# Token-major Wo and W2 products and a new order around W1 in an eight-layer attention stack

## Chip, cores, metric

One core of one Trainium2 chip. The metric is the device time of one execution in microseconds, the median over runs.

## The reference

x is 16 sequences of 128 tokens of 256. After a layer norm it goes through eight layers of linear attention and feed-forward, then a cross attention and a mixture of experts, which the change does not touch. All is float32. One layer:

```
Q  = elu(x Wq + bq) + 1;  K = elu(x Wk + bk) + 1;  V = x Wv + bv        (16 heads of 64)
KV = sum over tokens of K * V;  sumK = sum over tokens of K             (elementwise)
att = Q * KV / (Q * sumK + 1e-6)
y  = gelu(att Wo + bo);  x = layer_norm(y + x)                          (1024 -> 256)
h  = gelu(x W1 + b1);    h = gelu(h W2 + b2);  x = layer_norm(h + x)    (256 -> 1024 -> 256)
```

## The kernel before, in words

A tile is four sequences, 512 tokens; there are 4 tiles a layer and 8 layers, 32 tiles. Channels lie in chunks of 128 on the partitions ("feature-major", 128 x 512 tokens) or tokens lie on the partitions ("token-major", four blocks of 128 tokens x 256 channels). The Q, K, V and W1 products split operands into a high and a low part (float32r) and add three products per 128-channel half of the input (`split_product`, lines 328 to 334): high by high, high by low, low by high. The Wo and W2 products (`down`, line 377) are plain float32, which TensorE runs as two passes.

Work goes in slots, all engines with the same loop. Slot t finishes tile t (its Wo product, layer norm, W1), starts tile t+1 (Q, K, V for four pairs of chunks) and makes the W2 product of tile t-1. Each engine has its order written out by hand in its own function `slot` and waits on semaphores for the others:

- TensorE (line 402): pair 0 (K, Q, V), half of Wo's product, pair 1, its other half (`y_mm`), pair 2's K and Q, transposes of gelu(y) to token-major (`to_tm`, line 374), pair 2's V, half of W2's product, pair 3, most of its other half, transposes of the normed x into PS (line 448), the last three chunks of W2's product (`z_mm`), transposes of the input two tiles on (`input_fm`, line 365), W1's eight products (`hidden`), transposes of gelu(z). PS has six banks: two for K, two for Q, two for V; W1's products go round the last four, so that its fifth needs the first to be freed by ScalarE's gelu (`h_act`).
- ScalarE (line 565): per pair relu of K and Q (`clip_keys`, `clip_queries`) and one exponential over both (line 507), then Ln and exponential for the reciprocal (`invert`, lines 515, 517), then ATT from eight scaled pieces (`weigh`, line 530). Gelu needs another function table than Ln and exponential, so that a slot loads tables four times. Copies of the high parts: `X1HI` (line 594), `XTHI` (line 540).
- VectorE (line 715): per pair `features` (the snap of the exponential, line 625, then two K features, line 631, and two Q features, line 635), `sums_of` (two products by V, line 645, and a reduction, line 650), `denominators` (line 663), `newton` (lines 675, 677); for x the residual (line 693), statistics and `normed` (line 711), the low parts (lines 682, 687).
- GpSimd: rstd, scale and shift of both layer norms, and twelve weight pieces a layer that it splits in parts (lines 249, 251), in the slots with t = 2 and t = 4.
- SyncE issues all loads of the next layer as buffers come free.

## Time and profile before

| | |
|---|---|
| median of 3 runs | 3143.17 us (3138.88 to 3148.4) |
| the profiled execution | 3142.58 us |
| its span, first to last instruction | 3140.5 us |
| mean granted TensorE clock | 0.965 |
| TensorE, VectorE, ScalarE, GpSimd busy | 93%, 73%, 59%, 29% |

The attention stack takes the first 2580 us or so. Idle time of an engine is printed in brackets with the engine and line that ended it. A matmul's printed time holds the way through the array, so consecutive ones overlap; their spacing is the cost. "issue" means that the profile shows nothing the engine waited for.

### The profile page before, as it was taken

To read this page: it belongs to the slowest core of one execution; us is meant where nothing else is said; L and a number is where in the kernel's file an instruction comes from. 1 tells how busy PE (TensorE), PEld (TensorE's weight loads), DVE (VectorE), ACT (ScalarE), POOL (GpSimd) and SP (SyncE) were. 2 spreads that over 40 slices of the span, in tenths; PEclk is the share of its full clock that TensorE was granted. 3 is DMA by queue.
4 is the path that set the end of the run, shared out by engine and by line. 5 is a ranking of instruction groups with operands and counts; after the bars stand their busy time and mean duration, and the time that the engine had idled before them with its cause. 6 is when DMAs were issued, how large, how long until landed. Compare 5 with 4: busy or idle time off the path is not lost. (4 is left out here: it accounts for less than half of the span.)

```text
span 3140.5 us, 34598 instructions
## 1 busy us (share of the span) xinstructions
PE 2925.5 (93%) x11342; PEld 1984.7 (63%) x11343; DVE 2305.1 (73%) x3334; ACT 1863.0 (59%) x2796; POOL 922.0 (29%) x590
## 2 busy tenths in 40 slices
PE   5799999999999999999999989999999977997995
PEld 4566666566666666666666656666666635775563
DVE  6878888888887888788888788878787826763111
ACT  4566777677767776777677767776777713441121
POOL 5005231523152315231513151315131133323002
PEclk8899999999999999999999999999999988996998
DMA  4000000000000000100000000000000008000012
GB/s 129 1 1 26 28 17 19 27 28 17 19 26 28 17 19 27 28 17 19 27 28 17 19 26 28 17 19 26 28 17 4 0 1 273 0 0 22 14 45 77
DMA packets 59658, 92.82 MB, mean 30 GB/s; under 512 B 14960, under 2 KB 38768, under 8 KB 57424
## 3 DMA queue, kind: packets, MB, share of 16 engines
q1 hardware_dynamic: 56832, 83.27, 8.4%
q0 software_dynamic: 2640, 7.21, 0.7%
q8 instruction: 99, 1.62, 0.2%
q14 instruction: 87, 0.71, 0.1%
HBM read 80.24 MB, written 10.22 MB: 29 GB/s over the span
## 5 line engine op out<-in xcount | busy, mean ns | idle before, releaser
L331 PE MATMUL PS<-XTHI,WHI 128*128 128x512 f32 x1536 | 652.7, 425 | 47.9 <-DVE EX L631 32.7
L333 PE MATMUL PS<-XTHI,WLO 128*128 128x512 f32 x1536 | 611.8, 398 | 0.0
L332 PE MATMUL PS<-XTLO,WHI 128*128 128x512 f32 x1536 | 611.7, 398 | 0.0
L256 POOL TENSOR_TENSOR RSTD<-MV,EPS 128x4 f32<-128x4 f32 x68 | 41.2, 606 | 1529.6 <-DVE MV L703 1524.0
L381 PE MATMUL Y<-H,W2S 128*128 128x512 f32 x1024 | 461.2, 599 | 2.7 <-DVE R L693 2.7
L381 PE MATMUL Y<-ATT,WO 128*128 128x512 f32 x1024 | 451.7, 594 | 4.1 <-ACT ATT L530 2.7
L530 ACT ACTIVATE ATT<-INV,CC,CE 128x128 f32<-128x128 f32 x1024 | 425.0, 481 | 2.6 <-DVE INV L677 2.6
L331 PEld LDWEIGHTS PS<-XTHI,WHI 128*128 128x128 f32 x1536 | 293.2, 191 | 140.1 <-issue 56.0
L332 PEld LDWEIGHTS PS<-XTLO,WHI 128*128 128x128 f32 x1536 | 293.1, 191 | 83.1 <-issue 20.3
L495 ACT ACTIVATE EX<-PS,BNEG 128x512 f32<-128x512 f32 x256 | 169.8, 686 | 288.4 <-PE PS L333 286.1
L381 PEld LDWEIGHTS Y<-ATT,WO 128*128 128x128 f32 x1024 | 194.7, 190 | 226.2 <-issue 215.5
L333 PEld LDWEIGHTS PS<-XTHI,WLO 128*128 128x128 f32 x1536 | 292.5, 190 | 69.3
L381 PEld LDWEIGHTS Y<-H,W2S 128*128 128x128 f32 x1024 | 194.2, 192 | 212.8 <-issue 204.3
L650 DVE TENSOR_REDUCE SUMS<-EX 128x16 f32<-128x2048 f32 x128 | 292.4, 2284 | 3.3
L625 DVE TENSOR_SCALAR EX<-EX 128x2048 f32<-128x2048 f32 x128 | 224.0, 1750 | 49.8 <-ACT EX L507 49.8
L507 ACT ACTIVATE EX<-EX 128x2048 f32<-128x2048 f32 x128 | 245.3, 1916 | 4.1
L663 DVE TENSOR_TENSOR EX<-EX,ES 128x1024 f32<-128x1024 f32 x128 | 236.2, 1845 | 5.5
L675 DVE TENSOR_TENSOR EX<-EX,INV 128x1024 f32<-128x1024 f32 x128 | 165.0, 1289 | 96.9 <-ACT INV L517 96.7
L556 ACT ACTIVATE H<-PS,B 128x512 f32<-128x512 f32 x256 | 176.9, 691 | 79.5 <-PE PS L333 79.4
L331 PE MATMUL PS<-X1HI,W1HI 128*128 128x512 f32 x512 | 206.2, 403 | 0.0
L332 PE MATMUL PS<-X1LO,W1HI 128*128 128x512 f32 x512 | 202.9, 396 | 0.0
L333 PE MATMUL PS<-X1HI,W1LO 128*128 128x512 f32 x512 | 202.8, 396 | 0.0
(180 smaller groups left out, 4632.3 us busy)
## 6 DMA issues: line engine op xcount, KB each, us to landing
STAGE<-L_attn_Wkvq SPq DMA_DIRECT2D x64, 384.0 KB, 4.0
WO<-L_attn_Wo SPq DMA_DIRECT2D x8, 1024.0 KB, 4.9
W2S<-L_attn_W SPq DMA_DIRECT2D x8, 1024.0 KB, 4.8
STAGE<-L_attn_W SPq DMA_DIRECT2D x32, 256.0 KB, 5.1
WGU<-L_ffn_r_gate SPq DMA_DIRECT2D x8, 512.0 KB, 10.3
WGU<-L_ffn_r_up SPq DMA_DIRECT2D x8, 512.0 KB, 9.7
WD<-L_ffn_r_down SPq DMA_DIRECT2D x8, 512.0 KB, 10.2
rows_in<-ZERO SPq DMA_DIRECT2D x1, 2944.0 KB, 15.3
```

The source lines that it names most:

```text
L331: nc.tensor.matmul(out, whi[:, kc, :], xhi[:, kc, :], start=(kc == 0), stop=False)
L332: nc.tensor.matmul(out, whi[:, kc, :], xlo[:, kc, :], start=False, stop=False)
L333: ins = nc.tensor.matmul(out, wlo[:, kc, :], xhi[:, kc, :], start=False, stop=(kc == KD - 1))
L381: ins = nc.tensor.matmul(Yfm[:, m, :], w[:, c, m * P:(m + 1) * P], src[:, c, :], start=(c == 0), stop=(c == HC - 1))
L495: nc.scalar.activation(EX[:, b, 2 + i, :], PS[:, KB + i, :], ACT.Relu, scale=-1.0, bias=BNEG[:, 0, 2 * p + i:2 * p + i + 1])
L507: nc.scalar.activation(EX[:, b, 2:6, :], EX[:, b, 2:6, :], ACT.Exp, scale=-1.0).then_inc(ex, 1)
L530: ins = nc.scalar.activation(ATT[:, 2 * p + i, ss], INV[:, b, i, ss], ACT.Identity, scale=CE[:, b, k:k + 1], bias=CC[:, b, k:k + 1])
L556: nc.scalar.activation(H[:, m, :], PS[:, QB + m % 4, :], ACT.Gelu_apprx_tanh, bias=B1[:, m:m + 1]).then_inc(h_act, 1)
L625: nc.vector.tensor_scalar(EX[:, b, 2:6, :], EX[:, b, 2:6, :], -1.0, 1.0, ALU.add, ALU.add).then_inc(snap, 1)
L650: nc.vector.tensor_reduce(SUMS[:, b, :], by_seq(EX[:, b, 0:4, :]), AX.X, ALU.add).then_inc(sums, 1)
L663: nc.vector.tensor_tensor(q, q, spread(ES[:, b, :], SEQ), ALU.add).then_inc(denom, 1)
L675: nc.vector.tensor_tensor(EX[:, b, 4:6, :], EX[:, b, 4:6, :], INV[:, b, :, :], ALU.mult).then_inc(residue, 1)
```

## The change

- `down` makes the Wo and W2 products token-major: ATT or H is the stationary operand (a block of 128 tokens), the weights of 256 columns stream. Both groups of transposes (`to_tm`) go, with their semaphores.
- The biases BO and B2 become rows of 256, loaded to all partitions. VectorE adds them from PSUM into T (`biased`), ScalarE takes the gelu of T in place, in one instruction (`gelu_down`), and the residual reads T.
- W1's first two products begin with the two terms in X1's high part (`hidden_start`), then add the third (`hidden_rest`); the next input's transposes come behind them.
- z's gelu stands behind W1's first gelu; z's bias add inside the fourth pair's sums.
- On ScalarE the first pair's ATT comes ahead of y's gelu, the third pair's relus and exponential ahead of the second's Ln; on VectorE the second pair's newton comes behind the third's features.
- `features` snaps K's half and Q's half apart; X1's low part stands between the two halves of the third pair's newton; TensorE waits for each of the fourth pair's K features apart.

```diff
-            def to_tm(done, value, transposed):
-
-                pe.wait_ge(done, value)
-                for b in range(TS):
-                    for kc in range(KD):
-                        ins = nc.tensor.transpose(Ytm[:, b, kc * P:(kc + 1) * P], T[:, kc, b * P:(b + 1) * P],
-                                                  ident[:, :])
-                ins.then_inc(transposed, 1)
-
-            def down(w, src, m, chunks):
-
-                for c in chunks:
-                    ins = nc.tensor.matmul(Yfm[:, m, :], w[:, c, m * P:(m + 1) * P], src[:, c, :],
-                                           start=(c == 0), stop=(c == HC - 1))
+            def down(w, src, blocks, chunks=range(HC)):
+
+                for b in blocks:
+                    for c in chunks:
+                        ins = nc.tensor.matmul(Ytm[:, b, :], src[:, c, b * P:(b + 1) * P], w[:, c, :],
+                                               start=(c == 0), stop=(c == HC - 1))
                 return ins
 
-            def hidden(l, t, g):
+            def hidden_start(l, t, g):
 
                 if t == 0:
                     pe.wait_ge(w_lo, (l + 1) * PIECES)
                 chunks = (g + 2) * HC if exists(l, t + 1) else LAST * HC
-                for m in range(HC):
+                for m in range(2):
+                    pe.wait_ge(wq, chunks - 1 + m)
+                    for kc in range(KD):
+                        nc.tensor.matmul(PS[:, QB + m, :], W1HI[:, m, kc, :], X1HI[:, kc, :], start=(kc == 0), stop=False)
+                        nc.tensor.matmul(PS[:, QB + m, :], W1LO[:, m, kc, :], X1HI[:, kc, :], start=False, stop=False)
+
+            def hidden_rest(l, t, g, chunks):
+
+                last = (g + 2) * HC if exists(l, t + 1) else LAST * HC
+                for m in chunks:
                     if m < 2:
-                        pe.wait_ge(wq, chunks - 1 + m)
-                    elif m < 4:
-                        pe.wait_ge(kv_mul, chunks - 3 + m)
+                        for kc in range(KD):
+                            ins = nc.tensor.matmul(PS[:, QB + m, :], W1HI[:, m, kc, :], X1LO[:, kc, :], start=False,
+                                                   stop=(kc == KD - 1))
+                        ins.then_inc(h_mm, 1)
+                        continue
+                    if m < 4:
+                        pe.wait_ge(kv_mul, last - 3 + m)
                     else:
                         pe.wait_ge(h_act, g * HC + (m - 3))
                     split_product(PS[:, QB + m % 4, :], W1HI[:, m], W1LO[:, m], X1HI, X1LO).then_inc(h_mm, 1)
...
-                        pe.wait_ge(res2, g - 1)
+                        pe.wait_ge(z_b, g - 1)
                     if tt == 0:
                         pe.wait_ge(wo_in, (tl + 1) * 16)
                     pe.wait_ge(att, g * PAIRS + 3)
-                    down(WO, ATT, 0, range(HC - 2))
+                    down(WO, ATT, (0, 2), range(HC - 2))
                     pe.wait_ge(att, g * PAIRS + 4)
-                    down(WO, ATT, 0, range(HC - 2, HC))
+                    down(WO, ATT, (0, 2), range(HC - 2, HC))
...
-                    down(WO, ATT, 1, range(HC)).then_inc(y_mm, 1)
-                pair(2, 0, 2)
-                if tile:
-                    to_tm(y_act, g + 1, yt_mm)
-                pair(2, 1)
+                    down(WO, ATT, (1, 3)).then_inc(y_mm, 1)
+                pair(2, 0, 2, 1)
                 if before:
                     if tile:
-                        pe.wait_ge(res1, g + 1)
+                        pe.wait_ge(y_b, g + 1)
                     else:
-                        pe.wait_ge(res2, g - 1)
+                        pe.wait_ge(z_b, g - 1)
                      pe.wait_ge(h_act, g * HC)
-                    down(W2S, H, 0, range(HC))
+                    down(W2S, H, (0, 1))
                 pair(3, 0, 2, 1)
                 if before:
-                    ins = down(W2S, H, 1, range(HC - 3 if tile else HC))
+                    down(W2S, H, (2,))
+                    ins = down(W2S, H, (3,), range(4 if tile else HC))
                 if tile:
                     pe.wait_ge(x1, g + 1)
-                    if more:
-                        pe.wait_ge(kf, (g + 2) * HC)
                     for kc in range(KD):
+                        if more:
+                            pe.wait_ge(kf, (g + 2) * HC - 1 + kc)
                         for b in range(TS):
                             turn = nc.tensor.transpose(PS[:, KB + kc, b * P:(b + 1) * P],
                                                        R[:, t % 2, b, kc * P:(kc + 1) * P], ident[:, :])
...
-                        ins = down(W2S, H, 1, range(HC - 3, HC))
+                        ins = down(W2S, H, (3,), range(4, HC))
                 if before:
                     ins.then_inc(z_mm, 1)
                 if tile:
                     pe.wait_ge(x1_hi, g + 1)
+                    hidden_start(tl, tt, g)
                     pe.wait_ge(x1_lo, g + 1)
+                    hidden_rest(tl, tt, g, range(0, 2))
                 elif more:
                     pe.wait_ge(kf, (g + 2) * HC)
                 if exists(l, t + 2):
                     input_fm(g + 2, slot_of(l, t + 2)[1])
                 if tile:
-                    hidden(tl, tt, g)
-                if before:
-                    to_tm(z_act, g, zt_mm)
+                    hidden_rest(tl, tt, g, range(2, HC))
...
-            def gelu_down(mm, bias, bias_in, done, l, t, value):
-
-                if t == 0:
-                    act.wait_ge(bias_in, (l + 1) * 16)
-                act.wait_ge(mm, value)
-                for m in range(KD):
-                    ins = nc.scalar.activation(T[:, m, :], Yfm[:, m, :], ACT.Gelu_apprx_tanh, bias=bias[:, m:m + 1])
-                ins.then_inc(done, 1)
-
-            def hidden(l, t, g, between):
+            def gelu_down(biased, done, value):
+
+                act.wait_ge(biased, value)
+                nc.scalar.activation(T[:, :, :], T[:, :, :], ACT.Gelu_apprx_tanh).then_inc(done, 1)
+
+            def hidden(l, t, g, between, before):
                 if t == 0:
                     act.wait_ge(b1_in, (l + 1) * 16)
                 for m in range(HC):
                     act.wait_ge(h_mm, g * HC + (m + 1))
                     nc.scalar.activation(H[:, m, :], PS[:, QB + m % 4, :], ACT.Gelu_apprx_tanh,
                                          bias=B1[:, m:m + 1]).then_inc(h_act, 1)
+                    if m == 0 and before:
+                        gelu_down(z_b, z_act, g)
...
+                    weigh(nl, nt, 0)
                 if tile:
-                    gelu_down(y_mm, BO, bo_in, y_act, tl, tt, g + 1)
+                    gelu_down(y_b, y_act, g + 1)
...
                     clip_keys(nl, nt, 2)
+                    clip_queries(nl, nt, 2)
                     invert(nl, nt, 1)
-                    clip_queries(nl, nt, 2)
-                    weigh(nl, nt, 0)
...
-                if before:
-                    zl, zt = slot_of(l, t - 1)
-                    gelu_down(z_mm, B2, b2_in, z_act, zl, zt, g)
+                if before and not tile:
+                    gelu_down(z_b, z_act, g)
                 if exists(l, t + 2):
                     input_hi(g + 2)
                 if tile:
-                    hidden(tl, tt, g, (nl, nt, 2) if more else None)
+                    hidden(tl, tt, g, (nl, nt, 2) if more else None, before)
...
-                nc.vector.tensor_scalar(EX[:, b, 2:6, :], EX[:, b, 2:6, :], -1.0, 1.0, ALU.add, ALU.add).then_inc(snap, 1)
+                nc.vector.tensor_scalar(EX[:, b, 2:4, :], EX[:, b, 2:4, :], -1.0, 1.0, ALU.add, ALU.add).then_inc(snap, 1)
                 if t == 0 and b == 0:
                     dve.wait_ge(b_neg, 2 * l + (p // 2 + 1))
-                dve.wait_ge(snap, n + 1)
+                dve.wait_ge(snap, 2 * n + 1)
...
+                nc.vector.tensor_scalar(EX[:, b, 4:6, :], EX[:, b, 4:6, :], -1.0, 1.0, ALU.add, ALU.add).then_inc(snap, 1)
+                dve.wait_ge(snap, 2 * n + 2)
...
+                if biased2 is not None:
+                    z_biased(*biased2)
...
+                if between is not None:
+                    hidden_lo(between)
...
-            def residual(w, value, mm, add, res):
-
+            def biased(mm, value, bias, bias_in, layer, t, free, done):
+
+                if t == 0:
+                    dve.wait_ge(bias_in, (layer + 1) * 16)
+                if free is not None:
+                    dve.wait_ge(*free)
                 dve.wait_ge(mm, value)
-                nc.vector.tensor_tensor(R[:, w, :, :], Ytm[:, :, :], add, ALU.add).then_inc(res, 1)
+                nc.vector.tensor_tensor(T[:, :, :], Ytm[:, :, :], bcast(bias[:, :], TS), ALU.add).then_inc(done, 1)
+
+            def residual(w, value, gelu, add, res):
+
+                dve.wait_ge(gelu, value)
+                nc.vector.tensor_tensor(R[:, w, :, :], T[:, :, :], add, ALU.add).then_inc(res, 1)
...
+                if tile:
+
+                    biased(y_mm, g + 1, BO, bo_in, tl, tt, (res2, g - 1) if old else None, y_b)
...
-                    residual(w, g + 1, yt_mm, X[:, tt * TS:(tt + 1) * TS, :], res1)
-                if more:
-                    newton(nl, nt, 1)
-                if tile:
+                    residual(w, g + 1, y_act, X[:, tt * TS:(tt + 1) * TS, :], res1)
                     statistics(w, g + 1, mv1, res1, 0)
...
                     features(nl, nt, 2)
+                    newton(nl, nt, 1)
                     sums_of(nl, nt, 2, normed1=norm1)
 
                     denominators(nl, nt, 2)
                     features(nl, nt, 3)
-                    newton(nl, nt, 2)
-                    if tile:
-                        hidden_lo(g)
-                    sums_of(nl, nt, 3)
+                    newton(nl, nt, 2, between=g if tile else None)
+                    sums_of(nl, nt, 3, biased2=(l, t, g, tile) if before else None)
...
```

## Rows read from the trace of the kernel before

**Rows 1.** The page's first part: busy time, share of the span, instructions.

```profile
PE 2925.5 (93%) x11342; PEld 1984.7 (63%) x11343; DVE 2305.1 (73%) x3334; ACT 1863.0 (59%) x2796; POOL 922.0 (29%) x590
```

**Rows 2.** Timeline of TensorE, an ordinary slot: start, us, what, count, idle before.

```profile
1014.61 1.04 PE L448 MATMUL PS<-ident,R 128*128 128x128 f32 x8
...
1039.57 7.03 PE L381 MATMUL Y<-ATT,WO 128*128 128x512 f32 x16
...
1067.27 1.04 PE L374 MATMUL Y<-ident,T 128*128 128x128 f32 x8
...
1090.45 1.04 PE L448 MATMUL PS<-ident,R 128*128 128x128 f32 x8
...
1094.22 1.06 PE L365 MATMUL PS<-ident,X 128*128 128x128 f32 x8 [0.16 <-issue]
```

**Rows 3.** Spacing: split products (30 apart), then line 1367 and its weight loads.

```profile
1002.65 0.39 PE L331 MATMUL PS<-XTHI,WHI 128*128 128x512 f32 x1
...
1009.61 0.39 PE L331 MATMUL PS<-XTHI,WHI 128*128 128x512 f32 x1
...
2897.15 7.07 PE L1367 MATMUL PSX<-SD,HS 128*128 128x256 f32 x32
...
L1367 PEld LDWEIGHTS PSX<-SD,HS x128: 186/190/190, 2896.7 to 2963.2; 128*128 128x128 f32 x128
```

**Rows 4.** Timeline of ScalarE, the same ordinary slot.

```profile
1039.52 3.17 ACT L530 ACTIVATE ATT<-INV,CC,CE 128x128 f32<-128x128 f32 x8
...
1066.96 1.06 ACT L515 ACTIVATE INV<-EX 128x1024 f32<-128x1024 f32 x1
...
1070.30 1.91 ACT L507 ACTIVATE EX<-EX 128x2048 f32<-128x2048 f32 x1
...
1091.52 1.01 ACT L594 CAST X1HI<-PS 128x1024 fp32r<-128x1024 f32 x1 [2.95 <-PE PS L448]
```

**Rows 5.** Timeline of ScalarE, W1 of the first tile (no z yet).

```profile
157.96 1.02 ACT L540 CAST XTHI<-PS 128x1024 fp32r<-128x1024 f32 x1 [4.66 <-PE PS L365]
160.16 1.28 ACT L556 ACT_TABLE_LOAD   x1 [1.18 <-PE PS L333]
161.45 0.69 ACT L556 ACTIVATE H<-PS,B 128x512 f32<-128x512 f32 x1
...
162.43 0.67 ACT L556 ACTIVATE H<-PS,B 128x512 f32<-128x512 f32 x1
```

**Rows 6.** Timeline of VectorE, the ordinary slot of rows 2.

```profile
1069.56 1.22 DVE L675 TENSOR_TENSOR EX<-EX,INV 128x1024 f32<-128x1024 f32 x1
...
1073.68 1.19 DVE L625 TENSOR_SCALAR EX<-EX 128x2048 f32<-128x2048 f32 x1
...
1087.87 1.41 DVE L631 SCALAR_TENSOR_TENSOR EX<-PS,BUP,EX 128x512 f32<-128x512 f32 x2
...
1107.40 1.23 DVE L693 TENSOR_TENSOR R<-Y,R 128x1024 f32<-128x1024 f32 x1 [6.50 <-PE Y L374]
```

**Rows 7.** Timelines of TensorE, VectorE and GpSimd, two slots at a layer's end.

```profile
852.06 1.04 PE L448 MATMUL PS<-ident,R 128*128 128x128 f32 x8
...
902.29 0.50 PE L331 MATMUL PS<-XTHI,WHI 128*128 128x512 f32 x1 [2.25 <-DVE EX L631]
...
905.25 0.63 PE L331 MATMUL PS<-XTHI,WHI 128*128 128x512 f32 x1
...
934.38 1.09 PE L448 MATMUL PS<-ident,R 128*128 128x128 f32 x8 [1.47 <-DVE EX L631]
...
940.83 1.68 PE L365 MATMUL PS<-ident,X 128*128 128x128 f32 x8 [2.78 <-issue]
...
898.63 2.82 DVE L625 TENSOR_SCALAR EX<-EX 128x2048 f32<-128x2048 f32 x1
...
897.71 2.67 POOL L251 TENSOR_TENSOR WLO<-STAGE,WHI 128x768 fp32r<-128x768 f32 x1
```

**Rows 8.** Timeline of TensorE, the last tile's W2 product.

```profile
2532.05 12.94 PE L381 MATMUL Y<-H,W2S 128*128 128x512 f32 x26 [1.39 <-DVE R L693]
```

More of the change, by code:

```diff
@@ L80, in attention_stack @@
         BUP = sb("BUP", [P, 3, HC])
[L81 removed]
+        BO = sb("BO", [P, D])
         B1 = sb("B1", [P, HC])
[L83 removed]
+        B2 = sb("B2", [P, D])
         LN1P = sb("LN1P", [P, 2, D])
@@ L132, in attention_stack @@
             sem(n) for n in ("snap", "kf", "wq", "kv_mul", "sums", "stat", "denom", "residue", "recip", "xt_lo", "x1_lo"))
-        res1, mv1, x0, n1, res2, mv2, n2, mv0 = (
-            sem(n) for n in ("res1", "mv1", "x0", "n1", "res2", "mv2", "n2", "mv0"))
+        y_b, res1, mv1, x0, n1, z_b, res2, mv2, n2, mv0 = (
+            sem(n) for n in ("y_b", "res1", "mv1", "x0", "n1", "z_b", "res2", "mv2", "n2", "mv0"))
         half_set, w_hi, w_lo, r1, r2, xn_s, xn, r0 = (
@@ L191, in layer_loads @@
                 load_wide(WO, Wo, l + 1, wo_in)
-                sp.wait_ge(y_act, g)
-                load_fm(BO, bo, l + 1, bo_in)
+                sp.wait_ge(y_b, g)
+                load_row(BO, bo, l + 1, bo_in)
                 sp.wait_ge(x1, g)
@@ L201, in layer_loads @@
                 load_wide(W2S, W2, l + 1, w2_in)
-                sp.wait_ge(z_act, g)
-                load_fm(B2, b2, l + 1, b2_in)
+                sp.wait_ge(z_b, g)
+                load_row(B2, b2, l + 1, b2_in)
                 sp.wait_ge(xn, g)
@@ L669, in denominators, with newton @@
                 nc.vector.tensor_tensor(CE[:, b, :], CC[:, b, :], ES[:, b, :], ALU.mult).then_inc(stat, 1)
-            def newton(l, t, p):
+            def newton(l, t, p, between=None):
                 n, b = (l * TILES + t) * PAIRS + p, p % 2
@@ L713, in normed, with z_biased @@
                 ins.then_inc(done, 1)
+            def z_biased(l, t, g, tile):
+                zl, zt = slot_of(l, t - 1)
+                biased(z_mm, g, B2, b2_in, zl, zt, (res1, g + 1) if tile else (res2, g - 1), z_b)
             def slot(l, t):
@@ L719, in slot @@
                 tile, more = exists(l, t) and at_least(l, t, 0), exists(l, t + 1)
+                before = at_least(l, t, 1) and exists(l, t - 1)
                 old = at_least(l, t, 2)
@@ L722, in slot @@
                 if old:
-                    residual(w, g - 1, zt_mm, R[:, w, :, :], res2)
+                    residual(w, g - 1, z_act, R[:, w, :, :], res2)
                     statistics(w, g - 1, mv2, res2, 1)
@@ L734, in slot @@
                     features(nl, nt, 1)
+                if tile:
+                    biased(y_mm, g + 1, BO, bo_in, tl, tt, (res2, g - 1) if old else None, y_b)
+                if more:
                     sums_of(nl, nt, 1)
@@ L760, in slot @@
                     hidden_lo(g)
+                if before and not more:
+                    z_biased(l, t, g, tile)
                 if exists(l, t + 2):
@@ L791, in _ @@
                 features(0, 0, p)
+                if p > 1:
+                    newton(0, 0, p - 1)
                 sums_of(0, 0, p)
```

23 lines of the change are left out of this document (11 added, 12 removed).

## The prediction, made before the change was run

> **What bounds the kernel now.** I read the page first: TensorE is busy 93% of the span, VectorE 73%, ScalarE 59% [rows 1]. So a microsecond off an engine other than TensorE is worth nothing unless TensorE waits for it. Next I read TensorE's timeline over one slot (one tile's stage, from one start of the line 448 transposes to the next, 75.84 us) [rows 2]: in it only 0.16 us is idle, ahead of line 365. Then the slots at the end of a layer, in which GpSimd splits the next layer's weights: these two take 82.32 and 80.23 us [rows 7], 10.9 us above two ordinary ones. Named waits are 6.5 us of that (2.25 for the second pair's K, 1.47 ahead of the transposes, 2.78 ahead of line 365). Most of the rest is matmuls right behind a wait of over 2 us that run longer (0.63 instead of 0.39 us): at 1.2 instead of 2.4 GHz. Seven layers have such slots; the others are as the ordinary one.
>
> The time is therefore what TensorE has to stream, plus few waits. The sum is made against the profiled execution, 3142.6 us, 0.6 us under the median of the runs. A slot's events are counted below from X, the start of the line 448 transposes, and from H, the end of W1's last matmul; the next slot's first projection starts at H.
>
> **1. The transposes (line 374) go: -56 us.** Eight take 1.04 us with 0.27 us of tail in the last, so one costs (1.04-0.27)/7 = 0.11 us and eight 0.87 us [rows 2]. There are 64 such groups, 512 transposes. They lie on TensorE, the bound: 64 x 0.87 = 56.
>
> **2. 256 instead of 512 moving columns: +5 us.** An f32 product runs as two passes. Now 16 passes take 7.03 us with a 0.59 us tail: 0.429 us each [rows 2]; a slot has 64. After the change it has 128 of 256 columns. The same form stands on line 1367: 32 passes in 7.07 us with a 0.38 us tail, 0.2158 us each, with a 0.19 us weight load ahead of every one [rows 3]. 128 x 0.2158 - 64 x 0.429 = +0.16 us a slot, 32 slots. The Trainium skill (TensorE: Matmul & The Clock Gate, Measured speedup vs the span model) says that a weight load overlaps running matmuls only when its row group differs; by that rule 64 more full loads of 0.19 us would add 12 us to a slot, 390 us in all. The trace disagrees: line 1367's loads are of the full array and leave 0.0258 us between spacing and load.
>
> **3. VectorE: two bias adds, four more halves of a snap: hidden, 0 us.** An add from PSUM is 1.23 us (line 693's row), a snap of 2048 elements 1.19 us, so halves cost some 0.07 us more together [rows 6]: +2.8 us of VectorE a slot. It sat idle 6.5 us ahead of line 693 at the slot's end [rows 6], which is the cover. What is queued behind the new waits: y's bias add stands ahead of the second pair's sums and waits for y_mm, at H+30.7 (8.35 pair 0, 6.9, 8.35, 6.9). That holds sums, reduction and denominators back, which end at H+37.5, before ScalarE can give the third pair's exponential. That one I take from now: y_mm at 1061.8 (first half from 1039.57 [rows 2], 6.9 for it, 8.35 for pair 1, 7.0), exponential's end at 1072.21 [rows 4], 10.4 us later; minus the Ln and Exp moved behind it (2 x 1.06), plus the eight ATT pieces now ahead (3.1 [rows 4]; they wait for y_mm as well, since they overwrite ATT), minus 0.2 on the gelu: y_mm+11.1 = H+41.8. From there to the fourth pair's second K feature VectorE took 15.6 us (1073.68 to 1089.28), and now has 2.45 us of newton(1) more and 0.6 us of snap less: H+59.3. TensorE wants it at the fifth transpose, H+59.7. It fits by 0.4 us. Newton's half, then the X1 low part: X+4.4, wanted at X+4.5. The last V products: X+6.2 and X+6.9 against X+6.3 and X+7.6. All ties, so the bounds are 0 and +1.2 us a slot (one PSUM add late), +38 us; I take 0. The residual now reads two SBUF tensors: 1.22 us as line 675 [rows 6], 2.8 where GpSimd runs (line 625, [rows 7]), but GpSimd is idle at those two places.
>
> **4. W1 begun with X1's high part: 0 in ordinary slots.** Line 365 waited 0.16 us there [rows 2]. It is the start that buys nothing; what it displaces costs, see 5.
>
> **5. A new wait for ScalarE in W1: +24 us.** X1HI ends at X+2.08 [rows 2, 4]. TensorE: 0.87 transposes, 1.73 of z, 12 matmuls of 0.232 (2.78): the transposes of the next input now start at X+5.4 instead of before W1. ScalarE's order is X1HI, XTHI, W1's first gelu, z's gelu. XTHI starts at X+6.45 (1.07 behind, as X1HI) and ends at X+7.47. Only then comes the table load: in the first slot, where no gelu of z stands between, the load (1.28) is seen behind XTHI, and the gelu starts 0.01 us behind it [rows 5]. First gelu X+8.78 to 9.47; z's gelu (1024 from SBUF, 1.06 as line 515) frees ScalarE at 10.33; one ATT piece, second gelu 10.72 to 11.41; then one per 0.97 us (161.45 to 162.43 [rows 5]). TensorE wants bank 0 back at X+9.04 and gets it at 9.53; bank 1 at 10.92, gets it at 11.47. Wait 0.49 + 0.55 = 1.04 us. It applies to slots with a next input and without a longer VectorE wait, some 23: +24 us. Before, the load ran while TensorE finished z. Bounds: 0 (if the load slips ahead of XTHI) and 2 us a slot.
> The Trainium skill (ScalarE: Activation LUTs, What ACT_TABLE_LOAD costs) puts a switch at 2.66 us, a drain of 1.38 us beside the load; by that the wait would be 2.4 us, and the sum 32 us higher. The trace has no such drain behind a load, 0.01 us.
>
> **6. The two slots at a layer's end: -7 us.** The second pair's K waits for a snap that GpSimd holds up (2.82 us against 1.19 [rows 7]). Half the snap ahead of K gives back about 0.7 us, but TensorE arrives 1.3 us earlier and ScalarE, which ends W1 at its own pace of 0.97 us, 0.7 us later, so near 2 us of wait and its slow matmuls stay. The 1.47 us wait goes (K's features come singly). The 2.78 us wait becomes some 2.0 us inside W1 plus 1.2 us for the V products, since newton's second half and the low part run beside GpSimd. Net about -1 us a layer. Bounds: all of it gone, at most 76 us (7 x 10.9), or none and +7.
>
> **7. Ends: -5 us.** In the last slots TensorE waited for the residual (1.39 us [rows 8]) and now waits for the bias add only; ordinary idle 0.16 us goes once a layer. Biases as rows of 256 are small loads behind z_b and y_b on SP, needed a slot later: 0.
>
> Sum: -56 +5 +0 +0 +24 -7 -5 = -39, so 3142.6 - 39 = 3104 us, 1.2% faster. A measurement of this kernel can tell about 0.3%, 9.4 us.
>
> **Rivals.**
> A, the cover holds (0.22): ScalarE's load or the next input's transposes fall early enough, term 5 is 0, and part of the layer-end waits (10 us more) goes: about 3070. For it: ScalarE idles 2.95 us ahead of X1HI [rows 4]. Against: order is fixed, and the load stood behind XTHI.
> B, VectorE ends last (0.15): the ties of 3 break, TensorE waits 1.2 us more a slot at line 448, for X1LO or for the V products: 3142, no change. For: margins of 0.1 to 0.4 us. Against: 6.5 us of idle at the slot's end.
> C, slower (0.08): weight loads bound the shorter passes. The nearest other form is the split product, which streams half as many cycles a column yet is spaced 0.232 us (30 in 6.96 us [rows 3]) with the same 0.19 us load. At 0.232 a pass, 4096 passes cost 66 us more: 3170. It turns the sign from 0.2254 us a pass (39/4096 = 0.0095 over 0.2158). Against: line 1367 is the very form. The skill's overlap rule quoted in 2 is the extreme of this.
> My forecast itself has 0.55, with its own range 3085 to 3125.
>
> **Chances and range.** Faster 0.78 (forecast, A, 0.01 of B), within 0.3% 0.12 (B), slower 0.10 (C and 0.02 of B, ties broken by more than 1.5 us). The range 3052 to 3145 takes in A with half of term 6's bound and B as a whole; it leaves out C and the far ends, some 0.15.
>
> **What would show it.** Line 374 gone; line 381 with 4096 records spaced 0.216. TensorE idle of about 0.5 us twice in a slot, within W1's products, released by ScalarE's line of the hidden gelu; ScalarE's table load right behind XTHI. Ordinary slots near 75.2 us. y's bias add without a long wait at H+30.7, X1LO's end just before TensorE wants it. At the layer's end the second pair's wait still near 2 us. I am wrong if ordinary slots are at 74.2 (A), at 76 with idle time on VectorE's releases (B), or if line 381's spacing is over 0.22 (C).

## The result, and the profile after

| | before | after |
|---|---|---|
| median of 4 runs | 3141.65 us (3138.88 to 3148.4) | 3116.59 us (3113.95 to 3121.35) |
| ratio, 95% interval | | 0.9919 [0.9902, 0.9936] |
| the profiled execution | 3142.58 us | 3121.35 us |
| its span | 3140.5 us | 3119.4 us |
| mean granted TensorE clock | 0.965 | 0.962 |

The kernel is 25 us or 0.8% faster; the forecast was 39 us. The time lies in the range and above the forecast's own time by 13 us. It is within the forecast's own narrower range of 3085 to 3125, in part by luck, as the account below shows.

The page of after, its first part and the groups of the token-major products (columns: line, engine, operation, count | busy us, mean ns | idle before, what ended it):

```profile
PE 2888.2 (93%) x12878; PEld 2317.2 (74%) x12879; DVE 2397.5 (77%) x3526; ACT 1817.6 (58%) x2732; POOL 885.2 (28%) x590
...
L375 PE MATMUL Y<-W2S,H 128*128 128x256 f32 x2048 | 465.8, 384 | 2.3 <-DVE T L705 1.4
L375 PE MATMUL Y<-WO,ATT 128*128 128x256 f32 x2048 | 454.4, 380 | 5.2 <-ACT ATT L535 5.2
L375 PEld LDWEIGHTS Y<-WO,ATT 128*128 128x128 f32 x2048 | 389.8, 190 | 61.5 <-ACT ATT L535 4.1
```

Against [rows 1]: TensorE lost 37 us of busy time and VectorE gained 92. The 4096 passes of 256 columns are there (line 381 is now 375), the transposes of the products are not.

Next, TensorE's timeline of an ordinary slot of after (start, us, what, count, idle before), to be laid beside [rows 2]:

```profile
767.94 1.31 PE L453 MATMUL PS<-ident,R 128*128 128x128 f32 x8
...
772.42 0.40 PE L388 MATMUL PS<-X1HI,W1LO 128*128 128x512 f32 x1
772.91 1.21 PE L396 MATMUL PS<-X1LO,W1HI 128*128 128x512 f32 x4
773.95 1.03 PE L367 MATMUL PS<-ident,X 128*128 128x128 f32 x8
...
778.09 0.50 PE L333 MATMUL PS<-X1HI,W1HI 128*128 128x512 f32 x1 [0.34 <-ACT H L557]
...
780.00 0.51 PE L333 MATMUL PS<-X1HI,W1HI 128*128 128x512 f32 x1 [0.25 <-ACT H L557]
...
792.49 7.07 PE L375 MATMUL Y<-WO,ATT 128*128 128x256 f32 x32
...
843.17 1.20 PE L453 MATMUL PS<-ident,R 128*128 128x128 f32 x8
```

The slot takes 843.17 - 767.94 = 75.23 us, against 75.84. Three things to see. The product's 32 passes print 7.07 us, as line 1367's did [rows 3]. The first group of transposes prints 1.31 instead of 1.04 us: it stands 0.22 us in the middle, for the fourth pair's second K feature (spacings of 0.274 and 0.166 us there, 0.109 elsewhere). And W1 has the two forecast waits for ScalarE, 10.1 and 12.1 us after X. From 777.35 to 778.09 is 0.74 us where 0.23 is usual, so the first costs 0.51 us, the second 0.42; the brackets print only the part that the modelled ends leave over. The product behind each stop is spaced 0.34 us instead of 0.23 (778.09 to 778.43), which adds 0.11 each.

The same stretch on ScalarE:

```profile
769.29 1.01 ACT L597 CAST X1HI<-PS 128x1024 fp32r<-128x1024 f32 x1 [0.92 <-PE PS L453]
775.02 1.02 ACT L545 CAST XTHI<-PS 128x1024 fp32r<-128x1024 f32 x1 [4.72 <-PE PS L367]
776.06 1.28 ACT L557 ACT_TABLE_LOAD   x1
777.35 0.69 ACT L557 ACTIVATE H<-PS,B 128x512 f32<-128x512 f32 x1
...
779.27 0.67 ACT L557 ACTIVATE H<-PS,B 128x512 f32<-128x512 f32 x1
```

ScalarE is idle for 4.72 us, waiting for the transposes of the next input, and then begins XTHI; only behind that comes the table load of 1.28 us, with the gelu 0.01 us behind it, as in [rows 5]. TensorE waits for that gelu.

The slot at a layer's end, TensorE and then VectorE with GpSimd (to be laid beside [rows 7]):

```profile
843.17 1.20 PE L453 MATMUL PS<-ident,R 128*128 128x128 f32 x8
...
861.42 0.49 PE L333 MATMUL PS<-XTHI,WHI 128*128 128x512 f32 x1 [1.91 <-issue]
862.48 0.63 PE L334 MATMUL PS<-XTLO,WHI 128*128 128x512 f32 x1
...
925.71 1.31 PE L453 MATMUL PS<-ident,R 128*128 128x128 f32 x8 [3.44 <-DVE EX L633]
```

```profile
917.88 3.23 DVE L669 TENSOR_TENSOR EX<-EX,ES 128x1024 f32<-128x1024 f32 x1
921.03 1.42 DVE L672 SCALAR_TENSOR_TENSOR CC<-SUMS,ES 128x8 f32<-128x8 f32 x1
...
922.59 2.29 DVE L627 TENSOR_SCALAR EX<-EX 128x1024 f32<-128x1024 f32 x1
924.91 1.41 DVE L633 SCALAR_TENSOR_TENSOR EX<-PS,BUP,EX 128x512 f32<-128x512 f32 x2
...
917.65 2.37 POOL L302 TENSOR_TENSOR R<-R,LN1P 128x1024 f32<-128x1024 f32 x1
919.97 2.46 POOL L251 TENSOR_TENSOR WHI<-STAGE,ONE 128x768 fp32r<-128x768 f32 x1
922.51 1.81 POOL L253 TENSOR_TENSOR WLO<-STAGE,WHI 128x768 fp32r<-128x768 f32 x1
```

This slot takes 82.54 us, before 82.32. In it the wait for the second pair's K features (2.25 us before, ahead of the third pair's K product) is gone, but TensorE came there 1.91 us late from the start of its loop. The wait ahead of the transposes has grown from 1.47 to 3.44 us. The half snap takes 2.29 us instead of 0.69, and even an operation on 8 elements a partition 1.42 us instead of 0.15. Each of these VectorE instructions began while a GpSimd one ran, and ended only behind it (ends of GpSimd at 920.02, 922.43 and 924.32, of VectorE at 921.11, 922.45 and 924.88).

This is one of seven such slots, and they differ. Another of after, then the start of the transposes that ends the same tile's slot in before:

```profile
1481.76 0.50 PE L333 MATMUL PS<-XTHI,WHI 128*128 128x512 f32 x1 [1.35 <-issue]
1514.17 0.50 PE L333 MATMUL PS<-XTHI,WHI 128*128 128x512 f32 x1 [1.82 <-DVE EX L633]
1546.27 1.31 PE L453 MATMUL PS<-ident,R 128*128 128x128 f32 x8 [3.09 <-DVE EX L633]
```

```profile
1561.69 1.38 PE L448 MATMUL PS<-ident,R 128*128 128x128 f32 x8 [3.01 <-DVE EX L631]
```

In four of the seven first slots of after the wait for the second pair's K features still stands (1.70 to 2.44 us); in before it is 2.25 us in four and 0.38 in three. The wait ahead of the transposes is 3.09 to 3.44 us in all seven of after; in before it is 1.47 to 1.48 us in three and 2.99 to 3.02 in four, 16.5 us in all against 23.0. The slots of after take 81.2 to 82.6 us whichever of these waits they have.

Where the time went, from the starts of line 453 (448) in the two profiled executions, all 32 slots:

```
us                                        before   after   difference
start of the program to the first X        151.2   148.2   -3.0
first slots at a layer's end, 7            570.9   575.8   +4.9
second slots at a layer's end, 7           553.6   537.2  -16.4
ordinary slots, 16                        1216.4  1206.5   -9.9
last slot                                   52.6    50.0   -2.6
after the last X (mostly unchanged code)   595.7   601.7   +6.0
```

The last row is noise for the most part: over all kernels of this study that stretch took 592.6 to 602.4 us.

### The profile page after: what moved, and what is told of

Same layout as the page of the kernel before. It is cut to its first block and busy times, and to the rows that moved or that the text cites. A ratio compares the mean times of both kernels' runs of the same rounds, so it can differ in the third digit from the quotient of the medians.

```text
span 3119.4 us, 37809 instructions
## 1 busy us (share of the span) xinstructions
PE 2888.2 (93%) x12878; PEld 2317.2 (74%) x12879; DVE 2397.5 (77%) x3526; ACT 1817.6 (58%) x2732; POOL 885.2 (28%) x590
## 3 DMA queue, kind: packets, MB, share of 16 engines
HBM read 82.32 MB, written 10.22 MB: 30 GB/s over the span
## 5 line engine op out<-in xcount | busy, mean ns | idle before, releaser
L333 PE MATMUL PS<-XTHI,WHI 128*128 128x512 f32 x1536 | 625.8, 407 | 51.3 <-DVE EX L633 26.7
L375 PE MATMUL Y<-W2S,H 128*128 128x256 f32 x2048 | 465.8, 384 | 2.3 <-DVE T L705 1.4
L375 PE MATMUL Y<-WO,ATT 128*128 128x256 f32 x2048 | 454.4, 380 | 5.2 <-ACT ATT L535 5.2
L375 PEld LDWEIGHTS Y<-WO,ATT 128*128 128x128 f32 x2048 | 389.8, 190 | 61.5 <-ACT ATT L535 4.1
L375 PEld LDWEIGHTS Y<-W2S,H 128*128 128x128 f32 x2048 | 391.8, 193 | 58.4 <-DVE T L705 1.8
L258 POOL TENSOR_TENSOR RSTD<-MV,EPS 128x4 f32<-128x4 f32 x68 | 18.6, 274 | 1296.5 <-DVE MV L720 1290.9
L669 DVE TENSOR_TENSOR EX<-EX,ES 128x1024 f32<-128x1024 f32 x128 | 226.1, 1767 | 5.5
L520 ACT ACTIVATE INV<-EX 128x1024 f32<-128x1024 f32 x128 | 135.0, 1054 | 137.4 <-DVE EX L669 137.1
L627 DVE TENSOR_SCALAR EX<-EX 128x1024 f32<-128x1024 f32 x128 | 157.2, 1228 | 73.2 <-ACT EX L512 73.2
L633 DVE SCALAR_TENSOR_TENSOR EX<-PS,BUP,EX 128x512 f32<-128x512 f32 x256 | 180.4, 746 | 4.7
L639 DVE SCALAR_TENSOR_TENSOR EX<-PS,BUP,EX 128x512 f32<-128x512 f32 x256 | 180.4, 746 | 4.6
## 6 DMA issues: line engine op xcount, KB each, us to landing
WGU<-L_ffn_r_gate SPq DMA_DIRECT2D x8, 512.0 KB, 10.1
WD<-L_ffn_r_down SPq DMA_DIRECT2D x8, 512.0 KB, 10.1
```

Of the source, the lines that this page charges most:

```text
L333: nc.tensor.matmul(out, whi[:, kc, :], xhi[:, kc, :], start=(kc == 0), stop=False)
L375: ins = nc.tensor.matmul(Ytm[:, b, :], src[:, c, b * P:(b + 1) * P], w[:, c, :], start=(c == 0), stop=(c == HC - 1))
L633: nc.vector.scalar_tensor_tensor(EX[:, b, 2 + i, :], PS[:, KB + i, :], BUP[:, 0, c:c + 1], EX[:, b, 2 + i, :], ALU.add, ALU.max).then_inc( ...
L639: nc.vector.scalar_tensor_tensor(EX[:, b, 4 + i, :], PS[:, QB + i, :], BUP[:, 2, c:c + 1], EX[:, b, 4 + i, :], ALU.add, ALU.max).then_inc( ...
L669: nc.vector.tensor_tensor(q, q, spread(ES[:, b, :], SEQ), ALU.add).then_inc(denom, 1)
```

## Experiments

Each was made of the kernel after, unless said. Kernels run together share their runs of before; its median was 3145.67 us beside e1 to e4, 3141.98 beside e5 to e8, 3139.49 beside e9 to e12. Ratios are to before, so after's 0.9919 is what they are compared with. A difference of two ratios is turned into us with 3141.65. A difference by the medians takes 3116.59 for after and can be off by the up to 4 us by which the medians of before differ.

**e1: the table load placed by hand behind X1HI.**

```diff
                     nc.scalar.copy(X1HI[:, :, :], PS[:, KB:KB + 2, :]).then_inc(x1_hi, 1)
+                    nc.scalar.preload_act_table_set("gelu_apprx_tanh_and_others")
```

> The changed kernel with gelu's function table loaded right behind X1HI, ahead of XTHI. Theory (ScalarE's late load causes the two waits in W1, 0.51 + 0.42 = 0.93 us as the changed kernel's trace has them): both waits go, ordinary slots from 75.3 to about 74.4 us, and with the waits in some 28 slots 20 to 26 us less, 3091 to 3097 us. Rival (VectorE ends last: X1LO and the V products of the fourth pair come so late that TensorE waits for them instead): ordinary slots stay over 75.0 us and the time within 8 us of the changed kernel's 3117.

Measured: 3079.05 us, ratio 0.9788 [0.9771, 0.9805], 37 us by the medians and 41 us by the ratios under after; 20 to 26 had been expected. ScalarE, then TensorE, of an ordinary slot of e1:

```profile
759.53 1.01 ACT L597 CAST X1HI<-PS 128x1024 fp32r<-128x1024 f32 x1 [0.91 <-PE PS L453]
760.56 1.28 ACT L598 ACT_TABLE_LOAD   x1
765.25 1.01 ACT L545 CAST XTHI<-PS 128x1024 fp32r<-128x1024 f32 x1 [3.41 <-PE PS L367]
766.16 0.69 ACT L557 ACTIVATE H<-PS,B 128x512 f32<-128x512 f32 x1
```

```profile
758.18 1.31 PE L453 MATMUL PS<-ident,R 128*128 128x128 f32 x8
...
781.55 7.07 PE L375 MATMUL Y<-WO,ATT 128*128 128x256 f32 x32
```

The load lies in idle time, the gelu follows XTHI, and both waits in W1 are gone. X to the first Wo pass is 781.55 - 758.18 = 23.37 us, in after 792.49 - 767.94 = 24.55: 1.18 us a slot, the two waits (0.51 and 0.42) and the 0.11 behind each. 1.18 x 31 = 37 us, so the wait stood in every slot with a next input, those at a layer's end too. I had given it 1.04 us and 23 slots.

**e2 and e3: four weight pieces split half a slot later** (e2 on after, e3 on before). GpSimd's pieces 4 to 7 of W(K,V,Q) go from the end of slot t = 2 to behind the scaled input of slot t = 3.

```diff
+                if load and t == TILES - 1:
+                    for k in range(4, HC):
+                        split_piece(l + 1, k, False)
...
-                if load and t == TILES - 2:
-                    for k in range(4, HC):
-                        split_piece(l + 1, k, False)
```

> The changed kernel, with GpSimd's last four Q, K, V weight pieces split one slot later (first thing after the input's norm in the slot of the layer's last tile). Theory (in the slot before, VectorE is held up by GpSimd and sets its length, 82.4 us): the waits of 3.4 us ahead of line 453 go, that slot falls to some 78 us, and the time by 20 to 35 us, 3082 to 3097 us. Rival (the slot is long for its 1.9 us wait at the loop's jump and the slow matmuls behind it): 82.4 falls by less than 1.5 us, the time by under 10 us. What either costs in the later slot: 0 to 2 us a layer.

> The kernel before with the same move of GpSimd's pieces. Theory (the layer's end is set by VectorE and GpSimd in both kernels, so the change's savings on TensorE were lost there): it gains too, but less than the changed kernel does, 15 to 30 us (3112 to 3127), so that with the pieces late the changed kernel is 30 to 40 us ahead instead of 25. Rival (the layer's end took nothing from the change): both gain alike and the distance stays at 25 us.

Measured: e2 3109.99 us, 0.9887 [0.9868, 0.9905]; e3 3125.81 us, 0.9936 [0.9921, 0.9952]. So e2 gains 7 us on after by the medians and 10 by the ratios, whose intervals just touch, and e3 gains 20 us on before. The distance between the two kernels narrowed to 15 us by the ratios, where 30 to 40 had been expected. The first slots at a layer's end gained 19.3 us in e2 (575.8 to 556.5), and the second ones gave 11.7 back (537.2 to 548.9): the pieces meet VectorE there too. In e2's second slots TensorE waits for the second pair's K features:

```profile
660.62 0.50 PE L333 MATMUL PS<-XTHI,WHI 128*128 128x512 f32 x1 [2.05 <-DVE EX L633]
```

The expectation of 20 to 35 us for e2 fell. Moving the pieces moves the collision.

**e4: e1 and e2 together.**

> Both edits on the changed kernel. If the two waits are separate, the gains add: 3117 - 23 - 27 = about 3067 us (3055 to 3080). If VectorE's chain takes over once both are gone, the sum of the gains falls short by 10 us or more.

Measured: 3069.90 us, 0.9755 [0.9736, 0.9773]. 9 us under e1 by the medians, 10 by the ratios, as much as e2 gains on after. The two add up.

**e5: the start of W1 undone.** TensorE waits for X1's low part, transposes the next input, then makes all of W1.

```diff
                 if tile:
                     pe.wait_ge(x1_hi, g + 1)
-                    hidden_start(tl, tt, g)
                     pe.wait_ge(x1_lo, g + 1)
-                    hidden_rest(tl, tt, g, range(0, 2))
...
                     input_fm(g + 2, slot_of(l, t + 2)[1])
                 if tile:
+                    hidden_start(tl, tt, g)
+                    hidden_rest(tl, tt, g, range(0, 2))
                     hidden_rest(tl, tt, g, range(2, HC))
```

> The changed kernel with W1's early start undone: TensorE waits for X1's high and low part, transposes the next input, then makes all of W1. In the changed kernel's ordinary slot X1LO ends at X+4.9 while TensorE reaches the wait for X1HI at X+2.6. Theory: the start covers that wait of 2.3 us, at the price of the 0.93 us on ScalarE; undone, TensorE waits 2.3 us ahead of the input's transposes, the two waits in W1 go, ordinary slots from 75.3 to 76.2 to 76.7 us, the time by 25 to 45 us up. Rival (my prediction's step 4: the start buys nothing): the time falls, by up to 25 us, since the two waits go.

Measured, 12 runs: 3146.58 us, 1.002 [1.0006, 1.0034], 32 us over after by the ratios. TensorE of e5, an ordinary slot:

```profile
460.44 1.31 PE L453 MATMUL PS<-ident,R 128*128 128x128 f32 x8
...
465.45 1.06 PE L367 MATMUL PS<-ident,X 128*128 128x128 f32 x8 [1.97 <-issue]
```

Both waits in W1 are gone, and one of 1.97 us stands ahead of the input's transposes instead. Without the early start the whole gain of the change would be lost. By estimate only half of this price is the wait itself. After the first, the 15 ordinary slots of e5 all have it, but seven take 75.8 us and eight 77.4 to 77.8 (after: 75.1 to 75.5). Stretches of 5 us from the end of the wait in one slot of each kind, as `--windows` shows them (stretch and length, busy time of TensorE, its weight loads, VectorE, ScalarE and GpSimd with counts, granted clock, DMA):

```profile
703.40:708.40 5.00, 4.83 (x26) 4.14 (x27) 5.00 (x6) 3.69 (x4) 0.00 (x0) 1.00 0.01 2
779.20:784.20 5.00, 4.78 (x19) 3.96 (x20) 5.00 (x6) 2.30 (x2) 0.00 (x0) 0.66 0.48 196
```

In the longer kind part of the stretch ran at 1.2 GHz (mean granted clock 0.66) and TensorE made 19 matmuls instead of 26. Between the first and the last start of the transposes the clock stood at that level for 75.1 us in e5 and 44.4 in after (41.0 in before). At half speed the 31 us more cost some 15 us of the 32.

**e6: ScalarE's order undone.** y's gelu again ahead of the first pair's ATT, the second pair's Ln again ahead of the third's exponential.

```diff
-                    weigh(nl, nt, 0)
...
-                    clip_queries(nl, nt, 2)
                     invert(nl, nt, 1)
+                    clip_queries(nl, nt, 2)
+                    weigh(nl, nt, 0)
```

> The changed kernel with ScalarE's old order around y: gelu of y ahead of the first pair's ATT, the second pair's Ln and exponential ahead of the third pair's query relus and exponential. The Ln needs the second pair's denominators (VectorE, 5.9 us behind y_mm), so the third exponential ends about 1.0 us later than now. Theory (the chain third exponential, fourth pair's K features, transposes at line 453 is tight to 0.2 us): TensorE waits 0.8 to 1.2 us more in every slot, 25 to 35 us up. Rival (VectorE has room there): within 8 us of the changed kernel.

Measured: 3169.61 us, 1.0078 [1.0058, 1.0098], 50 us over after by the ratios, more than the 25 to 35 expected. In two ordinary slots of e6, TensorE ahead of the transposes:

```profile
468.20 1.31 PE L453 MATMUL PS<-ident,R 128*128 128x128 f32 x8 [1.51 <-DVE EX L633]
...
544.47 1.31 PE L453 MATMUL PS<-ident,R 128*128 128x128 f32 x8 [0.92 <-DVE EX L633]
```

The fourth pair's K is late in every slot, by 3.8 to 4.3 us at a layer's end. So the changed kernel needs ScalarE's new order. My reading is that y's bias add, which in token-major form stands in VectorE's queue ahead of the second pair's sums, is why; no run shows that by itself.

**e7: as many transposes again.** The transposes of the normed x are made three times, 16 more a slot.

```diff
-                        for b in range(TS):
+                        for b in list(range(TS)) * 3:
```

> The changed kernel with 16 more transposes a slot on TensorE (those of the normed x at line 453 made three times, the last ones stand). They cost 16 x 0.109 = 1.74 us of TensorE. Theory (TensorE bounds ordinary slots, VectorE the first slot at a layer's end): ordinary slots up by 1.6 to 1.8 us, the layer-end slot too as these stand behind its wait, 50 to 60 us up in all. Rival (another engine bounds, so that taking transposes away could give little): under 30 us up.

Measured, 12 runs: 3152.24 us, 1.0029 [1.0015, 1.0043], 35 us over after by the ratios, not 50 to 60. TensorE of e7:

```profile
701.22 2.84 PE L453 MATMUL PS<-ident,R 128*128 128x128 f32 x24 [0.16 <-DVE EX L633]
```

Slot by slot, the 14 ordinary ones that lie between layer ends take 76.5 instead of 75.35 us: +1.15 each where 16 transposes alone are 1.74. The rest is taken from waits. With 24 transposes TensorE is late enough for K's second feature (0.22 us) and for X1LO (0.26 us).

**e8: TensorE's loop over layers written out.**

```diff
-            with pe.Fori(0, LAYERS - 1, 1) as l:
+            for l in range(LAYERS - 1):
```

> The changed kernel with TensorE's loop over seven layers written out, so that TensorE makes no jump. Theory (the 1.8 us ahead of the first K product at the loop's start is the jump's fetch of instructions, and it moves the whole VectorE chain of that slot): the wait falls below 0.5 us, that slot from 82.4 to 80.0 to 81.0 us, and the time by 8 to 17 us. Rival (the wait is for the input's low part or another engine): that wait and the slot stay, within 5 us.

Measured: 3110.18 us, 0.9889 [0.9868, 0.9909], 6 us under after by the medians and 9 by the ratios; the intervals overlap, so the two are not told apart. TensorE of e8, a slot at a layer's end:

```profile
585.02 0.80 PE L333 MATMUL PS<-XTHI,WHI 128*128 128x512 f32 x1 [2.80 <-DVE EX L633]
...
617.23 1.22 PE L453 MATMUL PS<-ident,R 128*128 128x128 f32 x8 [1.93 <-DVE EX L633]
```

The 1.91 us ahead of the loop's body is gone, and in its place TensorE waits 2.80 us for the second pair's K features, for which it is now early. The seven first slots take 573.4 instead of 575.8 us, 81.9 on average where 80 to 81 had been expected. So the start of the loop is not what holds these slots long.

**e9 and e10: GpSimd's splits of W(K,V,Q) cut to one column** from the second layer on (e9 on after, e10 on before). Left out: those weights are not brought up to date, so all layers use those of the first layer. Instructions and waits stay.

```diff
+                if k < HC and not first:
+                    hi, lo, src = hi[:, 0:1], lo[:, 0:1], src[:, 0:1]
```

> The changed kernel with GpSimd's splits of the Q, K, V pieces cut to one column each from the second layer on (so these layers use the first layer's weights; all else is computed). Theory (the first slot at a layer's end, 82.3 us, is long because GpSimd's splits slow VectorE's instructions, and nothing else): it falls to 77 to 78 us (75.3 and the 1.9 us jump), the next from 76.7 to 75.3, the time by 38 to 50 us, to 3067 to 3079. Rival (the order of the changed kernel's own work sets it: y's bias add and the jump): it stays over 80 us and the time falls by under 20 us.

> The kernel before with the same cut. Theory: both of its slots at a layer's end go to 76 us (from 81.6 and 79.1), the time by 50 to 62 us to 3080 to 3092. It then gains more than the changed kernel does, and the distance falls from 25 to 10 to 17 us: the ordinary slots' 0.6 us times 32 minus the jump, so that the change's gain is in part a cheaper second slot at the layer's end. Rival (layer ends cost the change its savings): the distance grows to 35 us or more.

Measured: e9 3069.00 us, 0.9778 [0.9759, 0.9797]; e10 3086.44 us, 0.9834 [0.9815, 0.9852]. By the ratios e9 is 44 us under after and e10 52 us under before. VectorE and TensorE of e9 at the same place of a layer's end (lines are two higher than in after):

```profile
906.27 3.23 DVE L671 TENSOR_TENSOR EX<-EX,ES 128x1024 f32<-128x1024 f32 x1
909.42 0.15 DVE L674 SCALAR_TENSOR_TENSOR CC<-SUMS,ES 128x8 f32<-128x8 f32 x1
...
909.71 0.69 DVE L629 TENSOR_SCALAR EX<-EX 128x1024 f32<-128x1024 f32 x1
```

```profile
831.43 1.23 PE L455 MATMUL PS<-ident,R 128*128 128x128 f32 x8
...
850.73 0.50 PE L335 MATMUL PS<-XTHI,WHI 128*128 128x512 f32 x1 [2.92 <-issue]
...
911.33 1.23 PE L455 MATMUL PS<-ident,R 128*128 128x128 f32 x8
```

The small operation is back at 0.15 us and the half snap at 0.69; the wait ahead of the transposes is gone. The product of line 671 still takes 3.23 us, since the scale and shift of the layer norm still runs beside it. This slot is 79.90 us, with a wait of 2.92 us at the loop's start and slow matmuls behind it; another with the same wait takes 81.2. Four with a wait of 1.3 to 1.6 us there take 76.7 to 77.0, and the one outside the loop 75.1. The splits thus cost the kernel after 44 us and the kernel before 52. With both cut, the distance between the kernels is 18 us instead of 25 (10 to 17 had been expected).

**e11 and e12: what is to be had.** e11 is e1 with the four engines' loops over layers written out; e12 adds e2's later pieces.

> The changed kernel with gelu's table early and the layer loop written out on TensorE, ScalarE, VectorE and GpSimd. If the jumps of all four engines cost together what TensorE's alone gave (6 us), 3072 to 3076 us; if ScalarE's and VectorE's issue gaps of 1.0 and 1.8 us were what held the layer-end slot, that slot falls from 81.2 to 78 to 79.5 and the time to 3055 to 3068 us.

> All edits that gained: table early, four loops written out, last four pieces a slot later. Against e4's 3070 us it has the jumps gone: 3055 to 3064 us if they add, 3066 to 3072 if VectorE's chain at the layer's end takes them up, as it did when TensorE's loop alone was written out.

Measured: e11 3067.62 us, 0.9778 [0.9758, 0.9797]; e12 3063.18 us, 0.9759 [0.974, 0.9778]. e12 is 76 us or 2.4% under the before run beside it, and 1.6 points under after. Of that 1.3 points are e1's line. Beside e4 it is not told apart: 0.9755 and 0.9759. Writing the loops out gained 3 us on e1 by the ratios, within the intervals; e11's first slots at a layer's end still take about 80 us.

## Why the prediction was right, and where it was off

The sign, the likeliest case and the range held: the forecast's own range was 3085 to 3125. None of the rivals came as a whole, though B's ties broke by half a microsecond. The forecast was 13 to 14 us too low, and some of its steps missed by more than that and cancelled. One gain of some 21 us was in no step; without it the time would have been near 3138, outside the forecast's own range. That the number came so near is luck.

**Step 1, transposes, -56: not contradicted, its price not shown by itself.** They are gone. e7 put 16 others back, and 1.15 of their 1.74 us showed in ordinary slots; the rest covered two waits that the change had made. The stream shortened as worked, the waits are to be charged to step 3. At the six starts of the loop the eight transposes of z gave nothing by themselves. From W1's last product to the next K product, less the usual 0.23, it was 1.50 to 2.06 us in before (the transposes, then a wait of 0.47 to 1.03) and is 1.51 to 2.07 in after (wait alone).

**Step 2, shorter passes, +5: right.** After's ordinary product prints 32 passes in 7.07 us, as line 1367 does [rows 3], with loads of 0.19 us under a spacing of 0.216. Rival C falls. So does, for these loads, the rule of the Trainium skill (TensorE: Matmul & The Clock Gate, The mechanism) that a weight load overlaps running matmuls only when its row group differs: by it 390 us would have been added. The same section also lets a load into a background weight buffer run ahead, which the prediction left out (it also names another section for the rule). The 64 more loads a slot cost nothing here.

**Step 3, VectorE's ties, 0: partly broken.** I had K's second feature at H+59.3 against H+59.7, X1LO at X+4.4 against X+4.5. In after TensorE stands 0.22 us for the first and 0.26 us for the second (X1LO ends at X+4.9; VectorE's row is below). That is half a microsecond in an ordinary slot, 8 us in 16 of them, inside the bounds of 0 to 1.2.

```profile
771.63 1.22 DVE L695 TENSOR_TENSOR X1LO<-PS,X1HI 128x1024 fp32r<-128x1024 f32 x1
```

It starts at X+3.69 in the ordinary slot of after, and the product of line 396 goes on at X+4.97, where X+4.71 was due by the spacing ahead of it.

**Step 4, W1's early start, 0: right for the order of before, wrong for the new one.** Line 365 had waited 0.16 us [rows 2], which made me price the start at nothing. But in before X1LO ended at X+3.67 and z's products at about X+3.45; in after X1LO ends at X+4.91 and z's shorter part at about X+2.9. The start is what covers the gap. e5 gives it 32 us, about half of that by the lower clock behind the wait. I had priced the edit against the kernel before and not against the kernel without it.

**Step 5, the late table load, +24: the mechanism right, the term too small.** Order, place and releaser came as written. First gelu at X+9.41 instead of X+8.78, waits at X+10.1 and X+12.1. The waits are 0.93 us instead of 1.04, but with the late spacing behind each stop the price is 1.18 us a slot, and in 31 slots instead of 23: I had left out slots at a layer's end, assuming a longer VectorE wait there would hide it, but those waits stand elsewhere in the slot. e1 measures 37 us (41 by the ratios). Of the 2.66 us for a switch in the Trainium skill (ScalarE: Activation LUTs, What ACT_TABLE_LOAD costs) the load's 1.28 is seen and the drain is not: the gelu starts 0.01 us behind the load again.

**Step 6, a layer's end, -7: the step that failed.** For the 14 slots the steps add up to -22 us: -22 by steps 1 and 2, +7 by step 5 in the second slots, -7 here. Measured are -11.5 (+4.9 and -16.4). "The 1.47 us wait goes (K's features come singly)" is the wrong sentence: in all seven layers of after it stands at 3.1 to 3.4 us. I had read one of seven slots. In before the same wait was 3.0 us in four of them, and there the wait for the second pair was shorter in three. The 14 slots lay 62 us above ordinary ones, not the 76 (7 x 10.9) that I took as the bound.

And I let TensorE's way to the transposes get shorter without asking whether VectorE's could. From H to the start of the transposes it is 66.2 us in the slot of after shown above and 66.4 in that of before, where TensorE waited for both K features. To the end of the first alone it is 66.1 and 65.7. What the halved snap gave, GpSimd's pieces took (2.29 and 1.42 us in the rows above).

The rest of the forecast for this place held in part: near 2 us of wait for the second pair stayed in four slots of seven. e8 excludes the loop's start as the cause, and e9 shows GpSimd's splits to be it. With them cut, the wait is gone, and the slot is 5.5 to 6.2 us shorter in five layers, 1.0 and 2.6 us in the two with the long wait at the loop's start.

**Step 7, ends, -5: not confirmed.** The stretches outside the table's middle gained 3.0 and 2.6 us, but by the sum below some 3.5 of that is their share of the other steps. The reason given was wrong too: in the last W2 product the wait is as long as in [rows 8], now for the bias add. TensorE's timeline of after:

```profile
2505.48 12.35 PE L375 MATMUL Y<-W2S,H 128*128 128x256 f32 x56 [1.39 <-DVE T L705]
```

**Not in the forecast: the split products run closer together.** From TensorE's timeline of after, pair 1's products:

```profile
1049.86 0.39 PE L333 MATMUL PS<-XTHI,WHI 128*128 128x512 f32 x1
...
1056.72 0.39 PE L333 MATMUL PS<-XTHI,WHI 128*128 128x512 f32 x1
```

30 in 6.86 us are 0.2287, where before had 30 in 6.96 us [rows 3]. Over all split products between the first and the last X the mean spacing, waits left out, is 0.2326 us in before, e3 and e10, and 0.2291 to 0.2293 in after and in all ten experiments made of it. A slot has 192 such products (8 chunks each for Q, K, V and W1, six products a chunk), so 0.0034 us is 0.65 us a slot and 21 us in all, by estimate. This outweighs the miss it hid: without it the change would have been worth some 4 us. No single undoing (e5, e6, e7) brought the old spacing back, so neither W1's order nor ScalarE's nor the transposes' number makes it alone. Two things that all kernels made of after share were not undone: the token-major form, and the place of the operands in SBUF. BO and B2, declared ahead of XTHI, X1HI, ATT and H, grew from 2 to 256 columns, so that what comes behind them may lie elsewhere. The cause stays open.

**The sum by what was measured:** -56 + 5 + 8 (step 3) + 37 (step 5) - 21 (spacing) = -27. The 14 slots at a layer's end would have -14.7 of that (1.58 and 0.65 gained, 1.18 lost in each) and came to -11.5, so their own waits are about +3. With the 6.0 of the stretch after the last X, that is -18 against -21.2 between the profiled executions. The 3 us left are ordinary slots, which gained 1 more than this, and the ends with 2.

## What to carry to other kernels

Ask of each wait that an edit is to remove which engine's chain ends there, and whether that chain got shorter too; if only the waiting engine's did, the wait grows by what was saved. Where ScalarE changes its function table, the load stands at the first instruction of the new table, behind whatever that one's neighbours wait for; placed by hand in idle time it was worth 37 us here, more than the whole change. An edit that is worth nothing in the old order can carry the new one: price it by taking it out of the new kernel. A stage that repeats can differ from one repeat to the next: read the wait in all of them before pricing it.

## What was not expected of the hardware

- Some VectorE instructions that run beside a GpSimd one end only behind it, however small they are. 8 elements a partition took 1.42 us instead of 0.15 (line 672), a half snap 2.29 instead of 0.69 (line 627). Those that read PSUM kept their time (line 633: 0.75 us each in 81 cases under a GpSimd instruction and in 146 without), and so did the reduction (line 656, 2.28 us).
- TensorE stood 1.3 to 2.9 us at the start of its loop body over layers in after and e9, 0.5 to 1.0 in before (behind eight transposes), and not at all where the loop was written out (e8). In e5, with the loop kept, it stood 0.3 us at most. After 1.91 us of it the next matmuls printed 0.63 us instead of 0.39, the lower of the two clock levels (granted clock 0.66 over the 5 us from 861.5). After 1.83 us of it in another layer they did not.
- The spacing of the split products, 0.2326 and 0.2292 us in two families of kernels, with the same instruction form in both.
